# A graph layer with experts: GpSimd's small additions and loops taken out, the route's normalisation respaced, the output stored in seven large blocks

## The reference

```python
# x [6250, 256]; 100000 edges (row = src, col = dst, weight), sorted by col; 8 experts, 2 chosen
xn = layernorm(x)                                   # over the 256 columns
agg = segment_sum(edge_val[:, None] * xn[edge_col], edge_row)
gnn = agg @ W.T + b
q, k = elu(xn @ Wq.T) + 1, elu(...) + 1             # v = ...; 8 heads of 32
mix = (q @ (k.T @ v)) / max(q . sum(k), 1e-6)       # linear attention
x = x + gnn + (mix @ Wproj.T + bproj)
t = layernorm(x)
scores = t @ Wg.T + bg                              # [6250, 8]
top-2 per row, softmax over the two
x = x + sum over the two: p_e * (relu(t @ W1[e].T + b1[e]) @ W2[e].T + b2[e])
```

## Time and profile before

| | us |
|---|---|
| median of three runs | 2545.86 (2544.98 to 2547.69) |
| the profiled execution | 2546.2 |
| its span, first to last instruction | 2544.5 |
| PE busy in the span | 1667.6 (66%) |
| POOL busy | 1582.8 (62%) |
| DVE busy | 1469.4 (58%) |
| ACT busy | 1301.8 (51%) |
| mean granted clock of TensorE | 0.803 |
| DMA, mean over the span | 88 GB/s |

### The profile page before, as it was taken

One profiled execution on the slowest core, in us unless ns is written; L12 is line 12 of the kernel. 1 busy time (PEld: TensorE's weight loads), 2 busy tenths in 40 slices (PEclk: granted clock), 3 DMA queues, 4 the chain that ended last, 5 costly groups with the idle time before them and its releaser, 6 DMA issues. The chain is left out here.

```text
span 2544.5 us, 55005 instructions
## 1 busy us (share of the span) xinstructions
PE 1667.6 (66%) x13546; PEld 1204.8 (47%) x13546; DVE 1469.4 (58%) x3501; ACT 1301.8 (51%) x4202; POOL 1582.8 (62%) x1946
## 2 busy tenths in 40 slices
PE   6766445555565466666654434444638999999998
PEld 3555334443443345444442111111437777777776
DVE  7997435554554465555554554544874555555555
ACT  6454244454454455555544554554603666666665
POOL 3688846566566566666665666666535666666665
PEclk8998778787788688878876665555568999999999
DMA  4022144344344343333332223443601222223222
GB/s 139 22 79 68 49 133 128 115 124 119 117 126 120 116 116 98 98 97 97 97 89 75 83 82 103 138 135 89 202 12 48 47 48 47 46 48 49 47 47 33
DMA packets 140224, 224.35 MB, mean 88 GB/s; under 512 B 34054, under 2 KB 94672, under 8 KB 139954
## 3 DMA queue, kind: packets, MB, share of 16 engines
q0 software_dynamic: 67040, 146.22, 22.7%
q1 hardware_dynamic: 73042, 76.15, 9.7%
HBM read 181.40 MB, written 41.82 MB: 88 GB/s over the span
## 5 line engine op out<-in xcount | busy, mean ns | idle before, releaser
L973 POOL DMA_INDIRECT misc<-z_d,consts x902 | 860.5, 954 | 287.7 <-issue 285.2
L1225 DVE SCALAR_TENSOR_TENSOR acc<-ps,consts,acc 128x256 f32 x902 | 435.0, 482 | 603.7 <-remote 512.4
L1305 PE MATMUL ps<-misc 128*128 128x256 f16 x565 | 185.3, 328 | 375.3 <-DVE acc L1225 301.3
L1004 ACT ACTIVATE rec<-rec,misc 128x128 f16<-128x128 f16 x674 | 227.6, 391 | 207.4 <-DVE rec L1086 166.7
L1729 PE MATMUL ps<-misc,big 128*128 128x128 f16 x1680 | 327.9, 220 | 0.0
L1727 PE MATMUL ps<-misc,big 128*128 128x128 f16 x1680 | 327.7, 220 | 0.0
L1728 PE MATMUL ps<-misc,big 128*128 128x128 f16 x1680 | 327.5, 220 | 0.0
L1762 ACT ACTIVATE misc<-ps,misc 128x128 f32<-128x128 f32 x840 | 239.4, 368 | 160.1 <-PE ps L1729 145.7
L1743 PE MATMUL ps<-big,rec 128*128 x840 | 319.9, 381 | 1.5 <-DVE rec L1873 1.1
L1004 ACT ACTIVATE misc<-rec,misc 128x128 f16<-128x128 f16 x678 | 227.3, 391 | 161.9 <-DVE rec L1086 107.2
L739 POOL TENSOR_TENSOR consts<-consts 128x2 f32<-128x2 f32 x389 | 110.5, 284 | 313.8 <-PE ps L1307 154.8
(11 more groups left out here) (339 smaller groups left out, 4021.2 us busy)
## 6 DMA issues: line engine op xcount, KB each, us to landing
big<-in_w2T SPq DMA_DIRECT2D x60, 256.0 KB
misc<-z_d,consts POOLq DMA_INDIRECT x902
big<-xT_d SPq DMA_DIRECT2D x98, 128.0 KB
big<-in_w1T SPq DMA_DIRECT2D x32, 256.0 KB
tok_d<-misc SPq DMA_DIRECT2D x50, 132.0 KB, 1.9
xT_d<-misc SPq DMA_DIRECT2D x49, 128.0 KB
z_d<-misc SPq DMA_DIRECT2D x49, 128.0 KB
acc<-in_x SPq DMA_DIRECT2D x1, 6144.0 KB
```

Source lines behind the costliest of these rows:

```text
L973: e.indirect_dma_start(out=rows[k], out_offset=None, in_=c.z_d, in_offset=bass.IndirectOffsetOnAxis(ap=idx[u][:, k:k + 1], axis=0)).then_i ...
L1004: e.activation(hot[t % HG][:, half, :], same[t % OG], ACT.Copy, scale=near[t // UG][:, t % UG, 1 + half:2 + half]).then_inc(s_hot, 1)
L1225: e.scalar_tensor_tensor(out=rows_of, in0=out_ps[t % BG], scalar=c.gain, in1=rows_of, op0=ALU.mult, op1=ALU.add).then_inc(s_add[k], 1)
L1305: e.matmul(o, w[:, 0, :], rows[k][:, 0:D], start=True, stop=False)
```

## The change

Six edits:

- `carry` and its spare place are gone everywhere; a wait is followed by the indirect DMA itself.
- POOL's loops in the graph and in the experts are written out, and the experts' gathers and scatters read their column of the list in place: the 210 copies and one of the scatter's waits go.
- In the route, settle's small operations are put in four steps behind the norms 2 to 5 of a group; the seven measures come three, two and two behind the norms 0, 1 and 2; the inversion stands directly behind the norm 6, and a wait for VectorE's own queue ahead of each group's first norm; the score comes behind norm 4.
- `out` is stored by seven DMAs of up to seven tiles and one for the last 106 rows. ScalarE issues all eight at the route's start, ahead of its wait for the gate's weights. SP only stores tokens.
- The route's end no longer waits for stores: SP waits for the token stores ahead of the share store in the next block, VectorE for the first three large stores at that block's start, SP for the rest in the third block.
- The next block's scratch moves from `misc` to the part of `acc` that the first three stores have saved.

```diff
             def scatter(s):
                 e.wait_ge(s_what, s.i + 1)
-                carry(e, g, c.spare)
                 for n in range(KG):
...
-        def gather(e, g, q, u, tiles=UG):
+        def gather(e, q, u, tiles=UG):
...
                     if not first(q):
                         e.wait_ge(s_mm[k + QG - 1], q)
-                    carry(e, g, spare)
                 e.indirect_dma_start(out=rows[k], out_offset=None, in_=c.z_d,
...
-            g = Chain(e, s_g)
-            gather(e, g, 0, 0)
-            gather(e, g, 1, 1)
-            with e.Fori(1, LOOPS - 1) as j:
-                g.enter(j - 1, 2 * UG // QG)
-                for u in range(2):
-                    gather(e, g, j * 2 + u, u)
-            g.leave(LOOPS - 2)
-            gather(e, g, turns - 2, 0)
-            gather(e, g, turns - 1, 1, tiles_of(LOOPS - 1) - UG)
+            for q in range(turns - 1):
+                gather(e, q, q % 2)
+            gather(e, turns - 1, 1, tiles_of(LOOPS - 1) - UG)
...
             for i in range(NT):
-                rows = P if i < NT - 1 else TAIL
-                e.dma_start(c.out[i * P:i * P + rows, :], c.acc[0:rows, i * D:i * D + D]).then_inc(s_acc, 16)
                 e.wait_ge(s_lo, i + 1)
                 e.dma_start(c.tok_d[i * P:i * P + P, :], tok[i % TB].bitcast(F32)).then_inc(s_st[i % TB], 16)
             e.dma_start(c.tok_d[NP:NP + P, :], tok[(NT - 1) % TB].bitcast(F32)).then_inc(s_dump, 16)
-            e.wait_ge(s_acc, 16 * NT)
-            e.wait_ge(s_dump, 16)
-            for k in range(TB):
-                e.wait_ge(s_st[k], 16 * len(range(k, NT, TB)))
...
+            def settle(g, step):
                 v.sync()
+                if step == 0:
+                    v.add(e.tensor_tensor(x, q[:, :, 1], q[:, :, 4], ALU.subtract))
+                    v.add(e.tensor_tensor(m, q[:, :, 1], q[:, :, 4], ALU.add))
+                    v.add(e.tensor_tensor(q[:, :, 0], q[:, :, 2], q[:, :, 5], ALU.add))
+                elif step == 1:
+                    v.add(e.tensor_tensor(x, x, x, ALU.mult))
+                    v.add(e.tensor_scalar(m, m, 0.5, None, ALU.mult))
+                elif step == 2:
+                    v.add(e.tensor_scalar(x, x, 0.25, EPS, ALU.mult, ALU.add))
+                else:
+                    e.scalar_tensor_tensor(out=x, in0=q[:, :, 0], scalar=1.0 / D, in1=x, op0=ALU.mult,
+                                           op1=ALU.add).then_inc(s_var, 1)
...
+            AT = ((0, 1, 2), (3, 4), (5, 6), (), (), (), ())
             for i in range(NT):
+                g, n = i // GB, i % GB
+                if n == 0:
+                    v.sync()
                 norm(i)
-                if i + GB < NT:
-                    measure(i + GB)
-                if i % GB == GB - 1 and i < NT - 1:
-                    settle(i // GB + 1)
-                    invert(i // GB + 1)
-                if i % GB == 3 and i > GB:
-                    score(i // GB - 1)
+                if g < NT // GB - 1:
+                    for k in AT[n]:
+                        measure(g * GB + GB + k)
+                    if 2 <= n < 6:
+                        settle(g + 1, n - 2)
+                    if n == GB - 1:
+                        invert(g + 1)
+                if n == 4 and g > 0:
+                    score(g - 1)
...
+            for g in range(NT // GB):
+                full = GB if g < NT // GB - 1 else GB - 1
+                e.dma_start(c.out[g * GB * P:(g * GB + full) * P, :].rearrange("(t p) d -> p t d", p=P),
+                            c.acc3[:, g * GB:g * GB + full, :]).then_inc(s_acc0 if g < 3 else s_acc, 16)
+            e.dma_start(c.out[N - TAIL:N, :], c.acc3[0:TAIL, NT - 1, :]).then_inc(s_acc, 16)
             e.wait_ge(s_w, 32)
...
+    dead = Arena(c.acc, 3 * GB * D)
-    slots, after = matrix(misc.take(NE * NT), NE, NT), matrix(misc.take(NE * NT), NE, NT)
+    slots, after = matrix(dead.take(NE * NT), NE, NT), matrix(dead.take(NE * NT), NE, NT)
...
         def _(e):
             e.wait_ge(s_share, 1)
+            e.wait_ge(s_dump, 16)
+            for k in range(TB):
+                e.wait_ge(s_st[k], 16 * len(range(k, NT, TB)))
...
             v = Chain(e, s_c)
+            e.wait_ge(s_acc0, 16 * 3)
...
         def _(e):
+            e.wait_ge(s_acc, 16 * (NT // GB - 2))
             e.wait_ge(s_stored, 16)
...
             def gather(s):
-                g.add(e.tensor_copy(at[s.u], c.token[:, part_of(s.i, 1)]))
-                carry(e, g, c.spare)
...
-                                     in_offset=bass.IndirectOffsetOnAxis(ap=at[s.u][:, 0:1], axis=0)).then_inc(s_xs[s.u], 16)
+                                     in_offset=bass.IndirectOffsetOnAxis(ap=c.token[:, s.i:s.i + 1], axis=0)).then_inc(s_xs[s.u], 16)
             def scatter(s):
                 e.wait_ge(s_y, s.i + 1)
-                if not s.fresh:
-                    e.wait_ge(s_ys[s.u], 16 * s.j)
                 if not s.zero:
                     e.wait_ge(s_ys[1 - s.u], 16 * (s.j + s.u))
-                g.add(e.tensor_copy(to[s.u], c.token[:, bass.ds(s.i, 1)]))
-                carry(e, g, c.spare)
...
-            paired(e, MT - AHEAD, both, g, 4)
-            for i in range(MT - AHEAD, MT):
+            for i in range(MT):
                 scatter(Step(i // 2, i % 2))
+                if i + AHEAD < MT:
+                    gather(Step((i + AHEAD) // 2, i % 2))
```

More of the change, by code:

```diff
@@ L114, in build @@
         c.idx = [k.take(UG, I32) for _ in range(2)]
-        c.spare = k.take(8)
         c.valid = k.take(1)
@@ L498, in _ @@
             e.wait_ge(s_wlo, 1)
-            e.wait_ge(s_g, 16)
+            e.wait_ge(s_g, 15)
             v.link(e.tensor_copy(int1, place))
@@ L732, in paired @@
     body(Step(steps // 2, 0, False))
-def carry(e, g, spare):
-    g.sync()
-    g.add(e.tensor_tensor(spare[:, 4:6], spare[:, 0:2], spare[:, 2:4], ALU.add))
 def edges(c):
@@ L1351, in route @@
     s_score, s_half, s_wh, s_wl = S("score"), S("half"), S("gate_hi"), S("gate_lo")
-    s_st = [S(f"store{k}") for k in range(TB)]
+    s_st, s_acc0 = [S(f"store{k}") for k in range(TB)], S("acc_first")
     tr_ps = [matrix(c.bank[4 + u][:, 0:D].bitcast(F16), 2 * DH, P) for u in range(2)]
@@ L1382, in measure @@
                 v.add(e.bn_stats(st[:, i:i + 1, :], c.acc3[:, i:i + 1, :]))
-            def settle(g):
+            def settle(g, step):
                 part = slice(g * GB, g * GB + GB)
@@ L1398, in invert @@
                 e.wait_ge(s_std, g + 1)
-                v.link(e.reciprocal(rstd[:, part], std[:, part]))
+                v.add(e.reciprocal(rstd[:, part], std[:, part]))
             def norm(i):
@@ L1416, in _ @@
                 measure(i)
-            settle(0)
+            for step in range(4):
+                settle(0, step)
             e.wait_ge(s_wh, 1)
@@ L1464, in _ @@
                     turned_copy(i - 2)
-                if i % GB == GB - 1 and i < NT - 1:
+                if i % GB == GB - 1 and i < NT - GB:
                     deviation(i // GB + 1)
@@ L1504, in route @@
     ones16 = more.take(P, F16)
-    slots, after = matrix(misc.take(NE * NT), NE, NT), matrix(misc.take(NE * NT), NE, NT)
-    by_token = matrix(misc.take(NT * NE), NT, NE)
-    ones_row = misc.take(NE * NT)
-    slot_f = [misc.take(NT) for _ in range(TOP)]
-    last_e, past, tiles, ends, shift = (misc.take(NE) for _ in range(5))
-    tiles_i = misc.take(2 * NE, I32)
-    begun = matrix(misc.take(MT * (NE - 1)), MT, NE - 1)
-    order = misc.take(MT)
-    gap, ex, total = (misc.take(NT) for _ in range(3))
-    best = [misc.take(NT) for _ in range(TOP)]
+    slots, after = matrix(dead.take(NE * NT), NE, NT), matrix(dead.take(NE * NT), NE, NT)
+    by_token = matrix(dead.take(NT * NE), NT, NE)
+    ones_row = dead.take(NE * NT)
+    slot_f = [dead.take(NT) for _ in range(TOP)]
+    last_e, past, tiles, ends, shift = (dead.take(NE) for _ in range(5))
+    tiles_i = dead.take(2 * NE, I32)
+    begun = matrix(dead.take(MT * (NE - 1)), MT, NE - 1)
+    order = dead.take(MT)
+    gap, ex, total = (dead.take(NT) for _ in range(3))
+    best = [dead.take(NT) for _ in range(TOP)]
     rank_of = more.take(NE)
@@ L1696, in experts @@
     S = lambda name: c.sem("experts_" + name)
-    s_b, s_bias, s_bx, s_tr, s_xt, s_h, s_relu, s_high, s_low, s_out, s_y2, s_y, s_g = map(S, (
-        "b1", "bias", "b1_x", "tr", "xt", "h", "relu", "high", "low", "out", "y2", "y", "gpsimd"))
-    at, to = ([misc.take(1, I32) for _ in range(2)] for _ in range(2))
+    s_b, s_bias, s_bx, s_tr, s_xt, s_h, s_relu, s_high, s_low, s_out, s_y2, s_y = map(S, (
+        "b1", "bias", "b1_x", "tr", "xt", "h", "relu", "high", "low", "out", "y2", "y"))
     AHEAD = 6
@@ L1796, in gather @@
                     e.wait_ge(s_p, s.i - 1)
-                g.add(e.tensor_copy(at[s.u], c.token[:, part_of(s.i, 1)]))
-                carry(e, g, c.spare)
                 e.indirect_dma_start(out=xs[s.u].bitcast(F32), out_offset=None, in_=c.tok_d,
```

(16 more changed lines are left out.)

11 lines of the change are left out of this document (1 added, 10 removed).

## The result

The changed kernel takes 2529.82 us, the median of four runs (2524.35 to 2535.15), and the kernel before, run beside it again, 2546.78 (2544.98 to 2550.22): a ratio of 0.9935, with an interval of 0.9913 to 0.9957. That is 17 us faster, where I had forecast 33. The profiled execution took 2535.15 us, the slowest of the four, with a span of 2533.4; its stages say where the rest went.

The account below looks back on a forecast made before the run. POOL was taken to pace the sort, a closed POOL-PE-VectorE loop the graph, DVE the route, PE the experts. Sort -6, graph -30, route +4.5, experts -2 sum to -33.5 on 2546.2 us: 2513, range 2480 to 2552.

Parts of the forecast that it names:

- Sort: Edge sort: taking out the 27 carries between POOL's scatters gives -6 us, range -2.4 to -14.3.
- a good part is only moved: Edge sort: what blocks a carry beside VectorE can stretch the next scatter instead, so -6 us of at most 14.3.
- Graph: Graph stage: without 151 carries, POOL's loop of gathers and waits shortens; -30 us, range +25 to -60.
- 78 x 0.45 = 35: Graph stage: each of 78 runs of six gathers followed by a wait loses 0.45 us, together -35 us.
- if it follows POOL's start: Graph stage: the release comes about 8.5 us after a six-group's start; if tied to that start, the whole loop shortens.
- rival B: Graph stage: PE and VectorE set the release, so time is given back; graph -5, total about 2541 us; chance 0.20.
- Route (a): Route's start: ACT's eight output stores hold it 13.5 us and delay the first normalisation; +11.3 us, range +2 to +14.
- Route (b): Route's groups of seven tiles: respaced small operations make a group 7.4 us for 7.83; -2.6 us, range 0 to -6.
- Route (c): Route's end: SP's wait for stores goes behind the choice, so VectorE starts the next block earlier; -4.2 us.
- Experts: Experts stage: 210 copies and carries leave POOL, but only the ends count; -2 us, range -0.5 to -3.
- Rival D: Graph stage: groups of six gathers merge into twelve and the kernel gets slower, +16 us to 2562; chance 0.18.
- C: Whole kernel: sort gives 14 us, graph 50, ACT is blocked only 3.5 us; 2476 us; chance 0.10.

Follow-up runs that it names:

- sort_only: The kernel before with the carry taken out of the sort's 28 steps alone: 2236.97 us for 2249.50, ratio 0.9934.
- sort_memset: The kernel before with the sort's carry replaced by a memset of the same place, which reads nothing from SBUF: 2236.02 us for 2247.44, ratio 0.9947.
- after_dev: The changed kernel with ScalarE's square root moved ahead of the high half of a group's last tile: 2232.27 us; the kernel before 2249.43, ratio 0.9927.
- after_olddve: The changed kernel with VectorE's order in the route as before (settle, inversion, measures): 2229.14 us; the kernel before 2247.44, ratio 0.9926.

## Why the prediction was wrong

The forecast was 2513 and the time is 2529.8, inside the range; half of the forecast gain came. In the order of its steps:

- **Sort**, forecast -6 for -14.1 (first chip) and -12.5 (alone). The step that failed is "a good part is only moved" to the scatter: `sort_only` has the scatters' sum as it was. I had the price right (22.4 - 8.1 = 14.3) and discounted it for one long scatter. VectorE does hold scatters, 45 of 112 in the kernel before, but a scatter without a carry ahead of it waits for the operation that the carry waited for, and not for one more. The rule of the Trainium skill ("SBUF — State Buffer", section "Who interferes with whom") that I had set against the trace is borne out: the reading POOL instruction waits beside the two-input operations, the writing one (116 ns in `sort_memset`) does not, and the whole sum goes. My reading of it, that by this rule the carry alone is blocked, was wrong: the scatter reads its list of rows from SBUF, and it waits too.
- **Graph**, forecast -30 for -19.2. Here the largest error of the sum stands, the term 78 x 0.45 = 35 for the six-groups, which gave 5. Two steps of it failed. First the price: "each of the 78 six-groups can lose 0.35 to 0.6 us" took one price for two kinds of wait. It is 0.56 us ahead of a gather 6 and 0.13 ahead of a gather 0, 39 of each: 27 us. Second the overlap: "if it follows POOL's start, as it does in every six-group I looked at, the whole loop shortens". The release kept its 8.6 us in 71 of the 86 six-groups that I compare, but in 15 it came at 9.1 to 10.4 us, behind a product that was itself late. There the time is given back, the rival B that I gave 0.20. That the stage still gained 19 us is partly luck: 14 of them come from the twelve-groups, which I had put at "a few us". Why the counts come late on that chip at all was not settled: on four others the same code has no such waits, the carries cost 0.09 us each and the edit gives 12 to 14 us by that way.
- **Route (a)**, forecast +11.3 for +12.6: right, ScalarE held for 14.8 us against the 13.5 taken. The one queue row of the kernel's start was enough. The Trainium skill ("Perfetto Trace Analysis", section "DMA Instruction — HWDGE (DVE, Sync)") has each issue held until its own descriptors are made. The trace has the first two through in 0.44 and 0.57 us and only the later ones as long as a transfer (2.6). That speaks for a queue with room for about two such stores, whose issuer is held once it is full; the descriptors themselves are not in the trace, so it neither shows nor refutes the page's rule.
- **Route (b)**, forecast -2.6 for +4.3 (six groups of 8.54 for 7.83): the sign is wrong. "The deviation is early and its wait gone" is the failed step: I looked at VectorE's queue, where the settling is early, and not at ScalarE's, where the square root stands behind the last tile's high half and copy: VectorE waits 10.0 us for it over the route for 3.6 before. `after_dev` gets 1.9 us of the loss back, `after_olddve` 4.5, so the whole loss is the respacing's. The norms that meet POOL's low half are a second part, which the forecast did not have (25.8 us in all for 23.6 before). The terms of a group in the prediction also add up to 7.24 us and not to the 7.39 that the rows show; that changes nothing.
- **Route (c)**, forecast -4.2 for -4.5: right.
- **Experts**, forecast -2 for +9.8 on the first chip and -2.8 and -1.7 on two others, where neither can be told from none. The price was right where PE is undisturbed. On the first chip PE waits 0.12 us more in each tile for VectorE; that this has the same source as the late counts in the graph is an argument only, no run met such a chip again.
- **Rival D** (groups merge into twelve) did not come: 28 for 35. **C** was right in its first third, the sort.

The totals agree, -16.4 on another chip and -17.0 on the first, though the parts do not: the first chip gained some 6 us more in the graph and lost some 12 in the experts, by a profiled execution that was itself 5 us above its median. That the totals are alike looks like chance.

## What to carry to other kernels

Before an engine is given a batch of large transfers to issue, count what stands behind them in its queue: here eight issues held ScalarE for 14.8 us and put off the first normalisation by 12.6, while the same eight beside a stage that moved nearly nothing cost about 1 us. When small operations are moved earlier on one engine, follow their consumer's queue too: the square root was asked for earlier and done no earlier. Ask also what stands beside the moved operations on an engine that can hold them: the same norm took 0.40 us or 0.9, by whether it met POOL's subtraction. Price a wait at each place where it stands, since the kernel's text may have two waits at one and one at another. And a row that shows a cost in full (the carries' gaps) should be believed over a single row that could hide it.

## What was not expected of the hardware

- One kernel took 2546 us on one chip and 2247 to 2250 on four others, with the same loads and the same landing of rows (the last packet 2.4 us behind the issue). Nearly the whole difference is in the stage where POOL issues gathers all the time. In the six-groups of the kernel before, POOL's last gather ends 7.2 us after the start; of the 382 changes of PE's counts in these groups 196 stand in the ninth microsecond, though most of the products that raise them start in the first six. The counts of landed rows came together too: one buffer's is raised 1216 times, and the trace of the first chip has 223 changes of it, that of `sort_only` 1207. What makes it so stays open.
- A small POOL instruction takes 116 ns when it only writes and 648 ns on average when it adds two values that it reads, beside the same work of VectorE. The indirect scatters are held in the same way (1.61 to 2.79 us for 0.95 to 0.99).
- It goes the other way too: VectorE's norm of 0.40 us takes up to 0.9 when it meets POOL's subtraction, and then always ends 0.15 us behind it.
